# The squared terms of an expert's variance as high and low halves in rounded products

## The reference, cut to what matters

```python
logits = xf @ router_w                       # xf: layer-normed rows, 10000 x 512
gate_vals, idx = top_k(logits, 2); gates = softmax(gate_vals)
for e in range(8):
    h = relu(xf @ w1[e] + b1[e]) @ w2[e] + b2[e]          # 512 -> 32 -> 512
    y = (xf + h - mean) * rsqrt(var(xf + h) + 1e-6) * gamma[e] + beta[e]
    out = out + where(idx == e, gates, 0).sum(-1)[:, None] * y
```

## Time and profile before

| | us |
|---|---|
| median of 3 runs | 2734.81 (2732.6 to 2736.74) |
| the profiled execution | 2727.9 |
| its span (first to last instruction) | 2726.2 |
| PE busy | 2408.2 (88%) |
| DVE busy | 1765.9 (65%) |
| ACT busy | 1137.3 (42%) |
| POOL busy | 676.4 (25%) |

### The profile page before, as it was taken

One profiled execution on the slowest core, in us unless ns is written; L12 is line 12 of the kernel. 1 busy time (PEld: TensorE's weight loads), 2 busy tenths in 40 slices (PEclk: granted clock), 3 DMA queues, 4 the chain that ended last, 5 costly groups with the idle time before them and its releaser, 6 DMA issues. The chain is left out here.

```text
span 2726.2 us, 33928 instructions
## 1 busy us (share of the span) xinstructions
PE 2408.2 (88%) x10873; PEld 1874.7 (69%) x10876; DVE 1765.9 (65%) x4090; ACT 1137.3 (42%) x2072; POOL 676.4 (25%) x655
## 2 busy tenths in 40 slices
PE   5698919389999999999948999999989499999998
PEld 4465606277777777777836888888867377777776
DVE  7454277477777777777635675555556377777775
ACT  6453301244544544544324222222224566665651
POOL 5444400211211112111013122221222433333310
PEclk9799958699999999999979999999989699999999
DMA  4112001412212122121053334433336556666631
GB/s 138 47 32 48 16 4 58 152 42 89 79 61 93 61 79 93 51 89 62 24 167 119 127 119 150 133 129 130 130 114 195 122 130 142 165 143 164 139 109 47
DMA packets 156290, 272.16 MB, mean 100 GB/s; under 512 B 35634, under 2 KB 36274, under 8 KB 155894
## 3 DMA queue, kind: packets, MB, share of 16 engines
q1 hardware_dynamic: 122870, 202.74, 22.6%
q0 software_dynamic: 33280, 67.71, 10.7%
HBM read 186.35 MB, written 100.41 MB: 105 GB/s over the span
## 5 line engine op out<-in xcount | busy, mean ns | idle before, releaser
L1049 POOL TENSOR_TENSOR d_rs<-d_ve,net_half_neg 128x4 f32<-128x4 f32 x60 | 70.4, 1174 | 529.0 <-DVE d_ve L1105 428.5
L1984 ACT ACTIVATE conv_h<-conv_h 128x512 f32<-128x512 f32 x80 | 50.6, 632 | 311.4 <-DVE conv_h L1936 311.4
L2431 POOL DMA_INDIRECT next_own<-message,d_at x80 | 129.2, 1615 | 168.9 <-DMA next_own<-own 136.7
L1906 DVE TENSOR_TENSOR conv_yl<-conv_pty,conv_yh 128x512 fp32r<-128x512 f32 x80 | 55.3, 691 | 154.2 <-ACT conv_yh L1980 145.0
L65 PE MATMUL conv_p<-conv_w_hi,conv_yh 128*128 128x512 f32 x320 | 134.2, 419 | 0.6 <-DVE conv_yl L1906 0.6
L1062 POOL DMA_INDIRECT d_val<-values,d_at x80 | 86.0, 1076 | 192.2 <-DVE d_x L1187 172.0
L65 PE MATMUL d_po<-d_w_hi,d_hh 128*128 128x512 f32 x320 | 130.3, 407 | 2.5 <-DVE d_x L1200 0.4
L65 PE MATMUL d_pc<-d_xh,d_w_hi 128*128 128x512 f32 x320 | 131.5, 411 | 0.0
L65 PE MATMUL d_pa<-d_xh,d_w_hi 128*128 128x512 f32 x320 | 130.0, 406 | 0.3 <-DVE d_w_lo L1122 0.3
L1378 ACT ACTIVATE d_act_out<-d_pa 128x512 f32<-128x512 f32 x80 | 46.7, 583 | 199.2 <-PE d_pa L67 199.2
L65 PE MATMUL conv_p<-conv_w_hi,conv_hh 128*128 128x512 f32 x320 | 126.1, 394 | 2.0 <-DVE conv_hl L1906 1.9
(11 more groups left out here) (510 smaller groups left out, 7188.6 us busy)
## 6 DMA issues: line engine op xcount, KB each, us to landing
d_x<-in_x SPq DMA_DIRECT2D x20, 1024.0 KB, 7.0
y<-d_y SPq DMA_DIRECT2D x80, 256.0 KB, 2.0
conv_yin<-y SPq DMA_DIRECT2D x80, 256.0 KB, 2.8
h<-conv_h SPq DMA_DIRECT2D x80, 256.0 KB, 2.0
own<-conv_own SPq DMA_DIRECT2D x80, 256.0 KB, 2.0
next_own<-own SPq DMA_DIRECT2D x80, 256.0 KB, 4.9
next_x<-y SPq DMA_DIRECT2D x80, 256.0 KB, 3.0
out<-d_res SPq DMA_DIRECT2D x80, 256.0 KB, 2.6
```

The source lines that it names most:

```text
L1049: pool.tensor_tensor(rs[n][:], ve[n][:], k.half_neg[:, 0:T], ALU.pow).then_inc(pow_done[n], 1)
L1906: v.tensor_tensor(lo[:, t % 2, :], bank[t % 2][:], hi[:, t % 2, :].bitcast(F32), ALU.subtract)\
L1984: act_.activation(h[:, t, :], h[:, t, :], ACT.Relu).then_inc(h_made, 1)
L2431: pool.indirect_dma_start(own[n][:, t, :], None, k.message2[:, :], bass.IndirectOffsetOnAxis(ap=at[:, t:t + 1], axis=0), bounds_check=EP + ...
```

## The change

`quad` gets two halves of its own, `qh` and `ql`, in the rounded type. ACT makes `qh` by a copy (`quad_high`) in two new instructions per group, placed after `weighted_high(g - 1, 1)`: half 0 before the norm's squares of tiles 2 and 3, half 1 after them. DVE makes `ql = quad - qh` (`quad_low`), both halves after `weighted_low(g - 1, 1)` and ahead of `variance_of(g + 2)`. PE sums `qh` and `ql` in two rounded products per half, in place of one fp32 product per half, and waits for `ql` where it waited for `quad`.

```diff
-        hh, hl, ch, cl = (c.sb(n, [P, FC1, GR], F32R) for n in ("hh", "hl", "ch", "cl"))
+        hh, hl, ch, cl, qh, ql = (c.sb(n, [P, FC1, GR], F32R) for n in ("hh", "hl", "ch", "cl", "qh", "ql"))
...
+            def quad_high(g, fc):
+                act_.wait_ge(quad_made, FC1 * g + fc + 1)
+                act_.activation(qh[:, fc, :], quad[:, fc, :], ACT.Copy).then_inc(qh_made, 1)
...
                 if behind:
                     weighted_high(g - 1, 1)
+                if main:
+                    quad_high(g, 0)
                 if front:
                     square(i, c_ + 2, 2)
                     square(i, c_ + 2, 3)
+                if main:
+                    quad_high(g, 1)
                 if mid:
                     small_copy(g + 1)
...
+            def quad_low(g, fc):
+                v.wait_ge(qh_made, FC1 * g + fc + 1)
+                v.tensor_tensor(ql[:, fc, :], quad[:, fc, :], qh[:, fc, :].bitcast(F32), ALU.subtract).then_inc(ql_made, 1)
...
                 if behind:
                     weighted_low(g - 1, 1)
+                if main:
+                    quad_low(g, 0)
+                    quad_low(g, 1)
                 if front:
                     variance_of(i, c_ + 2)
...
                 for fc in range(FC1):
-                    pe.wait_ge(quad_made, FC1 * g + fc + 1)
-                    last = pe.matmul(psm[:], ex.expert[:, fc, :].bitcast(F32), quad[:, fc, :], start=alone and fc == 0,
-                                     stop=fc == FC1 - 1, skip_group_check=True)
+                    pe.wait_ge(ql_made, FC1 * g + fc + 1)
+                    pe.matmul(psm[:], ex.expert[:, fc, :], qh[:, fc, :], start=alone and fc == 0, stop=False,
+                              skip_group_check=True)
+                    last = pe.matmul(psm[:], ex.expert[:, fc, :], ql[:, fc, :], start=False, stop=fc == FC1 - 1,
+                                     skip_group_check=True)
```

More of the change, by code:

```diff
@@ L2363, in dense1_phase @@
         up_done, hid_made, hh_made, hl_made = (c.sem(n) for n in ("up_done", "hid_made", "hh_made", "hl_made"))
-        cross_done, quad_made = c.sem("cross_done"), c.sem("quad_made")
+        cross_done, quad_made, qh_made, ql_made = (c.sem(n) for n in ("cross_done", "quad_made", "qh_made", "ql_made"))
         route, exp_done, vars_, pow2_done, coefs = (c.sem(n) for n in ("route", "exp_done", "vars", "pow2_done", "coefs"))
```

## The result

The changed kernel takes 2768.8 us (median of 4 runs, 2766.2 to 2773.8) against 2735.8 us for the kernel before on the same chip (4 runs): ratio 1.0124, 95% interval 1.0107 to 1.0142. The forecast was +22.7 us and 2757.5 us with a range up to 2768; measured are +33 us, just outside it. The sign, the place and the size of the new wait are as forecast; a cost of some 10 us, which the forecast had put at nothing, came on top. It is lost while TensorE's granted clock is halved for short times.

What follows compares the result with a forecast made beforehand. PE, busy for all of the last stage's stretch, was taken as the bound. 17 x 1.28 = 21.8 us, group 19 +1.4, group 0 -0.5 and group 18 unchanged gave +22.7 on 2734.8: 2757.5 us, range 2747 to 2768.

Steps and rivals of the forecast that it cites:

- PE's own work: Last stage: four rounded products (0.93 us) replace four fp32 ones (1.71 us), relieving PE of 0.78 us a group.
- When the halves are ready: Squares of each group: PE waits for ql of half 1, 2.06 us waiting less 0.78 relief, 1.28 us later a group.
- The price of PE's start behind a wait: From the end of DVE's difference to the second product behind the wait on PE: 0.39 us.
- The ends of the stage: Groups outside the 1 to 17 pattern: group 18 no change, group 19 +1.4 us, group 0 -0.5 us.
- Nothing queued behind shifts by more: Small copy, variance, power, shifts and finish move with PE's delay in each group; no second delay is added.
- The sum: 17 groups at 1.28 us (21.8 us) plus the stage's ends give +22.7 us, 2757.5 us in all.
- the rival that PE's clock falls in the new wait: Half clock for 3.3 us a group: 1.6 us in each of 17 groups, 27 us more, 2785 us; 5 in 100.
- a lower clock as a sign of being wrong: A granted clock below 1.00 in the last stage's stretch of the profile after would show the forecast wrong.

Runs made afterwards that it cites:

- The products alone: Kernel before, with four rounded products a group reading hh and hl instead of fp32 products on quad; no new copy, difference or wait: 2713.9 us, ratio 0.9945.
- the filled run: Changed kernel with unread products in PE's waits, two ahead of the first half's sum and five ahead of the second's: 2750.2 us, ratio 1.0069 to the kernel before.
- the halves alone: Changed kernel's copies and differences kept, but PE sums quad in fp32 and waits for quad as before: 2729.6 us, ratio 1.0012 to the kernel before.
- both orders: Changed kernel with first-tile output products ahead of the squares on PE and the second qh copy ahead of the norm's squares on ACT: 2711.8 us, ratio 0.9944.
- the output tile alone: Changed kernel with PE's first-tile output products ahead of the squares and DVE finishing tile 1 earlier: 2722.5 us, ratio 0.9983 to the kernel before.

## Why the prediction was right in its chain and wrong in its sum

- **PE's own work** (0.78 us a group): right. The products alone show 0.78. The new products stand 0.23 to 0.24 us apart where PE doesn't wait; the 131 ns of the Trainium skill (TensorE: Matmul & The Clock Gate, Back-to-back issue gap) are not what any row here shows.
- **When the halves are ready**: right, in order and size. ACT's square, then the copy, then DVE's difference, then PE. +1.25 us in most groups at full clock, 1.27 on average over groups 1 to 17 of the filled run, against 1.28 forecast. That the two squares ahead of the copy decide is shown by moving it (27.61 us a group), and that the waiting and not the extra work costs, by the halves alone (27.61).
- **The price of PE's start behind a wait**, taken from another stage: 0.39 us forecast, 0.39 measured. One reading on the way was not borne out by its own row: that a difference starts 0.08 us before its neighbour on DVE ends. The trace after shows it (2446.48 against 2446.56), so it did no harm.
- **The ends of the stage**: right. The last group came out 1.4 us longer as forecast, group 18 unchanged (27.59), group 0 gained 0.7 where 0.5 was taken.
- **Nothing queued behind shifts by more**: right. A group at full clock holds nothing beyond the first delay. One time in it is misread, without effect: from the start of `variance_of` to the end of `shifts` the rows give 2.05 us (2420.58 to 2422.63), not 1.9.
- **The sum, and the rival that PE's clock falls in the new wait**: this step failed. The sum had no term for the clock; it took 1.00 throughout, and named a lower clock as a sign of being wrong. The sum of the forecast is 22.7 us, and the run with the waits filled shows +21.7 by its medians; the other 10 us are the clock. The rival was there, with its mechanism, but as all or nothing: it got 5 in 100 and the price of 17 groups, 27 us. What happens is that six of those groups are hit, at about 1.5 us each (9.2 / 6, near the 1.6 us worked out for one). Six times 1.6 on top of 22.7 are 32.3 us, where 33 were measured. So the price of one fall was right, and both the chance of any and their number were mis-judged. The evidence was read too kindly: the single wait of 1.80 us that kept the clock is no bound for two waits of some 2 us in all, close together and repeated 17 times.

The Trainium skill (same page, A second HAM failure mode: psum-queue depth-cycling) says that frequent short idles between groups of products can make TensorE's clock go back and forth. The change's traces agree: 1.00 and 0.50 by turns, six falls in some 495 us, each behind the waits at the squares. The forecast gave this little weight, because no row of the kernel before showed it.

What stays open is which groups are hit. In group 9 the same two waits, with PE as busy around them as in group 5, did not bring a fall:

```profile
2446.22:2449.63 3.41, 1.90 (x7) 0.94 (x6) 1.79 (x5) 2.06 (x6) 0.45 (x1) 1.00 0.14 25
```

So the waits make a fall possible and do not decide when. It is shown that filling the waits removes the falls, and that there are none where PE waits less: 3.2 us of idle time in eight groups with the copy moved ahead, against 12.1 in the change. The one wait in place of two brought more of them, by its length or by being in one piece.

The clock record adds one thing. Falls in neighbouring groups start 30.7 us apart in all three traces that have them: 2329.1, 2359.8 and 2390.6 us in the first, and from group to group in the run with one wait, where a group at full clock is half a microsecond longer. The two profiles of the change are hit in the same six of the 17 groups. This reads as if it matters when a wait comes and not only how long it is. No run moved the waits in time, so that is not shown.

## What to carry to other kernels

Work taken off the busiest engine is a gain only if what replaces it is ready there in time: follow the new chain through each engine's written order, because here two instructions that happened to stand in front of a short copy turned -15 us into +33, and moving one line brought the time back to that of the kernel before. The saving itself came through only when PE also had other ready work (an output tile) in the place of the wait that was left: -14.5 us with both orders, -3.7 with the output tile alone. Where a change brings repeated waits on TensorE, give a case its due in which the clock falls in some of the groups, and not only none or all.

## What the runs showed of the hardware that was not expected

TensorE got faster by doing more: with 7 products a group that nobody reads in its waits, PE's busy time in eight groups rose from 223.4 to 230.9 us and their length fell from 235.5 to 230.9, because the granted clock stayed at 1.00. And one wait in place of two ahead of the squares, with half a microsecond more of idle time, raised the number of falls from 6 to 16 in 17 groups and the cost of the change from 31.6 to 59 us.
